# Swapping the value and output projections within each attention step of a fused block

## The reference

```python
def proj(W):
    return jnp.einsum('btd,ed->bte', x, W).reshape(B, T, H, hd).transpose(0, 2, 1, 3)
q, k, v = _l2norm(proj(Wq)), _l2norm(proj(Wk)), proj(Wv)     # H = 16 heads of 16
attn = jnp.einsum('bhqd,bhkd->bhqk', q, k)
rel = pos[None, :] - pos[:, None]
mask = (rel < 0) | (rel >= 128)
alibi = -jnp.abs(rel) * slopes[:, None, None]
attn = softmax(where(mask, -1e30, alibi) + attn)
out = einsum('btd,ed->bte', attn @ v, Wo)
x = layernorm(x + out)
h = gelu(x @ (mean|w1| * sign(w1)).T + b1)
x = layernorm(x + h @ (mean|w2| * sign(w2)).T + b2)
```

## Time and profile before

| what | value |
|---|---|
| median of 3 runs | 370.71 us (370.42 to 370.77) |
| the profiled execution's own time | 370.34 us |
| its span | 368.5 us |
| TensorE busy | 354.0 us, 96% |
| VectorE busy | 324.2 us, 88% |
| ScalarE busy | 309.8 us, 84% |
| GpSimd busy | 273.2 us, 74% |
| mean granted clock of TensorE | 0.994 of full speed |

### The profile page before, as it was taken

How to read it: one execution, slowest core, us unless ns; L and a number is a source line. 1 busy time by engine, 2 the same in 40 slices (tenths; PEclk the granted TensorE clock), 3 DMA queues, 4 the chain that set the end, 5 groups by cost and what they waited for, 6 DMA issues and landing times. The chain is left out here.

```text
span 368.5 us, 13120 instructions
## 1 busy us (share of the span) xinstructions
PE 354.0 (96%) x4445; PEld 244.5 (66%) x4445; DVE 324.2 (88%) x857; ACT 309.8 (84%) x539; POOL 273.2 (74%) x418
## 2 busy tenths in 40 slices
PE   8799999999999999999999999999999999999991
PEld 6555676667767766776776667775666766766771
DVE  5978899898898898998889998869789999999995
ACT  2598898888898898898899999988888888887873
POOL 1189999889989999999999999756564664764321
PEclk9999999999999999999999999999999999999997
DMA  7668854844654655768766773303303413403113
GB/s 237 135 127 188 176 117 89 171 85 113 137 120 90 139 116 112 158 146 166 146 168 144 154 135 64 59 4 59 59 0 59 115 43 74 115 30 85 59 60 114
DMA packets 106885, 40.20 MB, mean 109 GB/s; under 512 B 92128, under 2 KB 105824, under 8 KB 106720
## 3 DMA queue, kind: packets, MB, share of 16 engines
q1 hardware_dynamic: 106848, 39.73, 48.5%
HBM read 12.72 MB, written 4.19 MB: 46 GB/s over the span
## 5 line engine op out<-in xcount | busy, mean ns | idle before, releaser
L1385 POOL TENSOR_SCALAR_AFFINE_SELECT prob<-prob 128x512 f32<-128x512 f32 x252 | 153.0, 642 | 11.3 <-ACT prob L692 11.2
L692 ACT ACTIVATE prob<-ps 128x1024 f32<-128x1024 f32 (+1 forms) x128 | 122.1, 1008 | 12.9 <-PE ps L388 12.9
L549 PE MATMUL ps<-yT,sgn 128*128 128x512 f16 x256 | 61.1, 379 | 0.0
L764 ACT ACTIVATE ps<-ps,bias,alpha 128x512 f32<-128x512 f32 x64 | 47.8, 750 | 15.8 <-PE ps L549 12.7
L419 PE MATMUL ps<-wqkv,xt 128*128 128x512 f32 x124 | 58.7, 596 | 1.4 <-DVE qkn L955 1.1
L1453 POOL TENSOR_TENSOR resid<-z,resid 128x256 f32 (+1 forms) x31 | 22.6, 730 | 46.1 <-DVE z L1182 46.1
L409 PE MATMUL ps<-prob,vdiag 128*17 128x128 f32 x1024 | 51.3, 274 | 0.2
L409 PE MATMUL ps<-prob,vnext 128*17 128x128 f32 x992 | 49.9, 273 | 0.0
L549 PEld LDWEIGHTS ps<-yT,sgn 128*128 128x128 f16 x256 | 25.0, 98 | 22.6
L452 PE MATMUL ps<-wo,oT 128*128 128x256 f32 x128 | 36.1, 404 | 0.1
L388 PE MATMUL ps<-qkT 64*64 64x192 f16 (+2 forms) x1024 | 33.8, 248 | 2.0 <-DMA qkT<-parts 1.4
(11 more groups left out here) (116 smaller groups left out, 684.8 us busy)
## 6 DMA issues: line engine op xcount, KB each, us to landing
xt<-in_xT SPq DMA_DIRECT2D x32, 128.0 KB, 2.1
resid<-in_x SPq DMA_DIRECT2D x32, 128.0 KB, 2.2
out_dram<-resid SPq DMA_DIRECT2D x7, 512.0 KB, 2.9
w<-in_w2T SPq DMA_DIRECT2D x1, 1024.0 KB, 8.2
w<-in_w1T SPq DMA_DIRECT2D x4, 256.0 KB, 3.3
w_nat<-in_w SPq DMA_DIRECT2D x4, 256.0 KB, 3.5
wqkv<-in_wqkvT SPq DMA_DIRECT2D x3, 256.0 KB, 3.7
qkT<-parts SPq DMA_TRANSPOSE x39, 4.3
```

What stands on the lines that cost most here:

```text
L549: mm = nc.tensor.matmul(ps[:, bank, :], sgn1[:, c, P * k:P * k + P], yT[:, par, a, c, :, :], start=(m == 0), stop=(m == 2 * DC - 1))
L692: nc.scalar.activation(to, scored, ACT.Exp, scale=QK_SCALE ** -2).then_inc(exp_done, 1)
L764: nc.scalar.activation(bank, bank, ACT.Gelu, bias=bias1[:, k:k + 1], scale=alpha1[:, k:k + 1]).then_inc(gelu_done, 1)
L1385: return nc.gpsimd.affine_select(out=at, in_=at, compare_op=ALU.is_ge, fill=0.0, base=-near, pattern=[[0, CH], [1 if near else -1, P]], ch ...
```

## The change

In a full step TensorE now makes the values of block i+1 where it made the outputs of block i-4, and the outputs where it made the values. VectorE fades the values directly behind `outputs`; the sums of squares come next, then the residual sum and the layer norm, and the copy stays last. The turned rows get two buffers, chosen by parity. The wait on the layer-norm seed moves from VectorE's `sums_of` to ScalarE's `norm_of`. Steps 0 to 3 and 29 to 31 keep their order. There are 25 full steps (4 to 28). In them the value projection waits for the residual sum of block i-5, and the output projection for the fades of block i+1.

```diff
-        oT = sb("oT", [P, DC, P])
+        oT = sb("oT", [P, 2, DC, P])
...
-            def project_v(n, slot):
+            def project_v(n, slot, added=None):
 
                 count(pe, v_ready, n)
-                count(pe, resid_done, n - 4)
+                count(pe, resid_done, n - 4 if added is None else added)
...
-            def project_out(q, values, added=0):
+            def project_out(q, at, values, added=0):
 
                 pe.wait_ge(ot_ready, q + 1)
                 pe.wait_ge(v_ready, values)
...
-                    mm = nc.tensor.matmul(ps[:, VO, D:2 * D], oT[:, k, :], wo[:, k, :],
+                    mm = nc.tensor.matmul(ps[:, VO, D:2 * D], oT[:, at, k, :], wo[:, k, :],
...
-                if out:
-                    project_out(i - 4, i + 1)
+                full = out and next1 and next3
+                if full:
+                    project_v(i + 1, (slot + 1) % XS, i - 4)
+                elif out:
+                    project_out(i - 4, par, i + 1, i - 4)
...
-                if next1 and next3 and not early:
+                if full:
+                    project_out(i - 4, par, i + 2)
+                if next1 and next3 and not full and not early:
                     project_v(i + 1, (slot + 1) % XS)
...
-            def take_rows(q):
+            def take_rows(q, at):
                 act.wait_ge(ot_done, q + 1)
-                count(act, wo_done, q)
+                count(act, wo_done, q - 1)
...
-                if not next3:
+                if ln:
                     act.wait_ge(ln_seed, i - 3)
...
-            def sums_of(n, ln):
+            def sums_of(n):
...
-                if ln:
-                    dve.wait_ge(ln_seed, n - 6)
...
                     outputs(i - 3)
-                if out and next3:
-                    add_output(i - 4)
...
+                if next3 and not double_first:
+                    fade_values(i + 1, (slot + 1) % XS)
                 if prev_ln:
                     y_row(i - 5, prev3)
+                if next3:
+                    sums_of(i + 3)
+                    if out:
+                        add_output(i - 4)
                 if ln:
                     layer_norm(i - 4)
...
-                if next3:
-                    sums_of(i + 3, ln)
-                    if not double_first:
-                        fade_values(i + 1, (slot + 1) % XS)
                 if next2:
                     double(i + 2, par)
```

More of the change, by code:

```diff
@@ L599, in _ @@
             pe.wait_ge(prep, 1)
-            project_out(NB - 4, NB)
+            project_out(NB - 4, 0, NB)
             turn_bound()
@@ L608, in _ @@
                 weighted_sum(NB - 2, c, 2)
-            project_out(NB - 3, NB, NB - 3)
+            project_out(NB - 3, 1, NB, NB - 3)
             turn_strips(NB - 2)
@@ L615, in _ @@
                 weighted_sum(NB - 1, c, 3, near=False)
-            project_out(NB - 2, NB, NB - 2)
+            project_out(NB - 2, 0, NB, NB - 2)
             turn_strips(NB - 1)
@@ L620, in _ @@
             hidden(0, 7, 0)
-            project_out(NB - 1, NB, NB - 1)
+            project_out(NB - 1, 1, NB, NB - 1)
             for b, chunks in enumerate(((0, 1, 2), (3, 4), (5, 6), (7,))):
@@ L667, in take_strips @@
                                      ACT.Copy).then_inc(strips_ready, 1)
-            def take_rows(q):
+            def take_rows(q, at):
                 act.wait_ge(ot_done, q + 1)
-                count(act, wo_done, q)
-                nc.scalar.activation(oT[:], ps[:, OT, 0:D].rearrange("p (k t) -> p k t", k=DC),
+                count(act, wo_done, q - 1)
+                nc.scalar.activation(oT[:, at, :, :], ps[:, OT, 0:D].rearrange("p (k t) -> p k t", k=DC),
                                      ACT.Copy).then_inc(ot_ready, 1)
@@ L706, in step @@
                 if strips:
-                    take_rows(i - 3)
+                    take_rows(i - 3, 1 - par)
                 if squares_first:
@@ L811, in _ @@
             gelu_of(0, 0, 0)
-            take_rows(NB - 3)
+            take_rows(NB - 3, 1)
             gelu_of(0, 1, 0)
@@ L820, in _ @@
             high_hidden(0, 3, 0)
-            take_rows(NB - 2)
+            take_rows(NB - 2, 0)
             gelu_of(0, 4, 0)
@@ L826, in _ @@
             gelu_of(0, 6, 0)
-            take_rows(NB - 1)
+            take_rows(NB - 1, 1)
             high_hidden(0, 6, 0)
@@ L1051, in take_bound @@
                 nc.vector.tensor_reduce(bound_max[:], turned_at, AX.X, ALU.max).then_inc(bound_max_done, 1)
-            sums_of(0, False)
+            sums_of(0)
             round_of(-3, True, False)
             normalise_rows(0, 0)
-            sums_of(1, False)
+            sums_of(1)
             split_keys(0)
@@ L1060, in _ @@
             dve.wait_ge(first_low, 1)
-            sums_of(2, False)
+            sums_of(2)
             split_keys(1)
@@ L1067, in _ @@
             abs_w2(0, P)
-            sums_of(3, False)
+            sums_of(3)
             double(2, 0)
@@ L1074, in _ @@
             fade_values(2, 2)
-            sums_of(4, False)
+            sums_of(4)
             double(3, 1)
@@ L1079, in _ @@
             abs_w2(P, P + P // 2)
-            sums_of(5, False)
+            sums_of(5)
             double(4, 0)
@@ L1085, in _ @@
             fade_values(3, 3)
-            sums_of(6, False)
+            sums_of(6)
             fade_values(4, 0)
```

## The result

The changed kernel takes 378.26 us (median of 4 runs, 377.44 to 378.68), the kernel before 370.74 us beside it: a ratio of 1.0208, 95% interval 1.0193 to 1.0223. Predicted were 376.9 us, 370.5 to 382. Direction and size hold. The working behind them holds only in part, as the experiments show.

The account below looks back on a forecast made before the run. Bound: TensorE's own work (7.08 us a step) and, within 0.1 us, a ring through TensorE, ScalarE and VectorE. Loop 4.6 plus last five steps 1.65 made 6.3 us, 376.6 from 370.34; with 0.37 for the median, 376.9 us, range 370.5 to 382.

Parts of the forecast that it names:

- The ring through the fades: Second scores wait behind the output projection for two fades instead of one residual sum: 0.23 us per loop step, 4.6 us.
- The 7.18 of the prediction: Time of a loop step in the kernel before, from four steps in 28.72 us; the loss was counted from it.
- rival A: Newton round escapes GpSimd and its operations shorten, so the kernel gets faster by 3.0 us, 367.7; 9% together with another rival.
- The last five full steps: The five full steps behind the loop lose the whole 0.33 us each by the longer wait, 1.65 us.
- the floor: Shortest step that TensorE's own work alone allows, taken as 7.08 us.
- VectorE's rear: Later residual sum, statistics, seed and copy before the next Newton round: 0.1 to 0.6 us of slack in most steps, cost 0.
- the wait of ScalarE's logarithm: ScalarE waits for the layer-norm seed, now just before the copy: the same slack less the copy's 0.65 us, cost 0.
- rival C: VectorE's late work delays the Newton round by 0.4 us in every step: a further 9 us, 386 us; 18% from 380 upwards.
- The loads: SyncE's load of xt goes some 3.4 us earlier, for a step far ahead; nothing waits for it, cost 0.
- The turned rows' two buffers: The second buffer removes a wait that was not late: costs and gives nothing, but is needed in the new order.
- The wait by bank: Outputs cannot be written while fades read the values' half of the same PSUM bank, so the new wait is real.

Follow-up runs that it names:

- e4: Kernel before, order untouched, with the residual sum's operation done twice in each of the 25 full steps: 374.77 us, ratio 1.0114.
- e5: Changed kernel with layer-norm statistics of the full steps taken ahead of the sums of squares and residual sum, so of other numbers: 375.38 us, ratio 1.0104.
- e1: Changed kernel with outputs of the 25 full steps written to the query/key bank VectorE has just finished reading: 372.18 us, ratio 1.0036.
- e12: Changed kernel with loads of xt and resid held until the same step's output projection from block 9 on, measured beside the changed kernel: 375.86 us.
- e9: Changed kernel with loads of xt and resid held until the same step's output projection is done, from block 9 on: 376.34 us, ratio 1.0158.
- e10: Kernel before with two buffers for the turned rows and nothing else: 370.49 against 370.48 us, ratio 1.0004.
- e8: Changed kernel with one buffer for the turned rows instead of two: 379.61 us, ratio 1.0239.
- e7: Kernel before, in its order, with values of the 25 full steps projected into the query/key bank VectorE has just finished reading: 369.15 us, ratio 0.9963.
- e6: Changed kernel with both the edits of e1 and e5: 368.10 us, ratio 0.9923.
- e2: Changed kernel with the second fade computed from the first one's result in SBUF, not from PSUM: 382.04 us, ratio 1.0311.

## Why the prediction was right, and where it was not

**The ring through the fades: right in its mechanism, counted too dear.** The load stands 0.12 us behind the second fade, and four steps of e4 take 7.38 us in the mean against 7.41 forecast. But the 20 loop steps lose 3.3 us in e4 (148.71 against 145.43) where 4.6 were forecast. The 7.18 of the prediction does not hold for all twenty: the first five took 7.53 us each before and grew by 0.09, the others took 7.19 and grew by 0.19. And the Newton round got shorter, 1.34 us for its three operations in the mean of e4's loop and 1.26 in the changed kernel's, 1.41 before: rival A, in small. The changed kernel's four steps take 30.22 us where I had said 29.6; with the four ahead of them it is 59.70 us for eight, 7.46 a step. The excess is the rear's: with the statistics first, eight steps take 58.57 us (e5). Without the wait for the fades 6.1 us are gone (e1).

**The last five full steps: 1.65 us forecast, 2.4 measured, for another reason.** The ring alone gives 0.9 us there (e4). My 0.33 a step was the whole distance of two operations. In e4 the five steps grow by 0.26, 0.19, 0.05, 0.32 and 0.07 us; the first two stood at the floor before, and why two others hardly grow stays open. Most of the rest goes with the early loads: with them back in place the five steps take 36.73 us in e12's profile, 0.34 above the kernel before, but 37.67 in e9's.

**VectorE's rear: costed at 0, wrong.** This is the step of the prediction that failed. I gave it 0.1 to 0.6 us of slack in most steps and let only the worst meet the round 0.4 us late. e5 puts it at 2.9 us, 2.2 of them in the loop. Two terms were mis-sized. I let the sums follow y_row at once, while they wait up to 0.40 us for squares that ScalarE makes only when queries and keys are projected. And the seed took up to 1.18 us, beyond the 0.86 of the earlier trace rows (0.71 in the mean of the loop, 0.46 before): in 12 of 22 steps it now starts 0.03 to 0.26 us behind the start of GpSimd's second low-half operation (1.16 us) and ends with it. In the kernel before it started 0.35 us or more behind that start, as at 104.83 us against 104.36, where it took 0.74. I had also named the wait of ScalarE's logarithm and dismissed it in one sentence, though it comes before the copy of the strips and so reaches TensorE by a second way. My rival C was this mechanism; it acted at a third of its 9 us, beside the ring and not in its place. SBUF — State Buffer of the Trainium skill, section "SBUF: two separate sides", says that the loser of the shared port pair blocks until the other's instruction is over; the ends at 107.94 and 107.90 agree.

**The loads: costed at 0, wrong by about 2 us in the median.** I asked whether something waits for the load, and not what the load gets in the way of.

**The turned rows' two buffers: right** that they give nothing in the old order (e10). In the new one they may be worth 1.35 us (e8), none of it in the loop.

**The wait by bank: as forecast.** Products wait for reads of columns that they do not touch, and moving either product to a bank that is free at that time takes the wait away (e1, e7). The wait is a semaphore of the program, so the runs show its price and not what the chip would do without it. Its being there is in line with PSUM — Partial Sum Buffer of the Trainium skill, section "PSUM bank collisions raise a hardware error"; whether columns alone would do was not tried.

**The sum.** Ring 4.0 (e4), rear 2.9 (e5), loads about 2 (e12) make 8.9 for 7.5 us. The parts are not additive: where one wait is longer, another is hidden behind it. By stretch, in us, each from one profile:

| kernel | median | 20 loop steps | last five full steps |
|---|---|---|---|
| before | 370.74 | 145.43 | 36.39 |
| changed | 378.26 | 150.12 | 38.78 |
| e4, ring alone | 374.77 | 148.71 | 37.28 |
| e5, no late rear | 375.38 | 147.88 | 38.73 |
| e1, no wait for the fades | 372.18 | 145.10 | 37.72 |
| e6, neither | 368.10 | 143.26 | 35.79 |
| e12, late loads | 375.86 | 150.08 | 36.73 |

In the loop, where the loads cost nothing, ring and rear make 3.3 + 2.2 = 5.5 for 4.7 us. In the other direction e1 takes 5.0 us off the loop, e5 2.2, and both together 6.9, less than the sum, because both end at the same floor. Over the whole kernel it is 6.1, 2.9 and 10.2, more than the sum. Of that, 1.1, 0.1 and 3.0 us lie in the last five full steps, where e1 and e5 each have a stop without a releaser and e6 has none. The forecast of 6.3 us was near by luck: a ring counted 2.3 us too dear stood in for a rear and loads counted as nothing.

What stays open: why TensorE stands still behind the loop with the early loads, and what else varies there.

## What to carry to other kernels

When two products change places, count the instructions that the later one now waits for on the reader's engine, and then do the same for everything that this engine does afterwards: the operation pushed to its rear may close a second ring. If a product waits only because it shares a PSUM bank with data that it does not touch, look for a bank that is free at that moment before reordering anything; here that was worth more than the order (369.15 us). A transfer issued earlier is not free because nothing waits for it: compare the steps behind a loop as well as those in it. And before two savings are added up, look stretch by stretch whether they end at the same floor.

## What the runs showed of the hardware

An operation of VectorE on 32 columns took 0.18 us where it started less than 0.1 us before the end of GpSimd's (68.72 us in the kernel before, GpSimd done at 68.80), and 1.17 us where it started 0.03 us behind the start of one of 1.16 us. A fade from PSUM took 0.41 to 0.43 us in every step, the same shape from SBUF 0.42 to 0.99, 0.87 in the median (e2). From the end of VectorE's last read to the start of a weight load that waits for it there are 0.12 us, before and after. Behind the loop TensorE stops for 0.5 to 1.7 us with no releaser in six of eight profiles with early loads, and in none of six with late ones.
